# Local output projection moved into the feed-forward pipeline, its neighbours' weights loaded and folded at other points

## The reference

```python
# local attention: o = per-head attended values (4, 1024, 512), window of 128 tokens
x = layernorm(x + (o @ Wo.T + bo))                 # its output projection
# strided cross attention: 16 heads, 4 keys per head and batch, out of the 64 context rows
x = layernorm(x + strided_attention(x, ctx))
# feed-forward with blockwise FP4 rounding q() of input, hidden and weights, 512 -> 1408 -> 512
h = silu(q(x) @ q(w_gate).T) * (q(x) @ q(w_up).T)
x = layernorm(x + q(h) @ q(w_down).T)
```

## Time and profile before

| | us |
|---|---|
| median of 3 runs | 3055.73 (3054.52 to 3055.9) |
| profiled execution, its own time | 3053.7 |
| its span | 3052.0 |
| PE busy | 2701.3 (89%) |
| DVE, ACT, POOL busy | 1879.7, 846.6, 724.7 |
| last PE instruction of `local_attention` starts | 1748.6 |
| projection's first and last matmul start | 1772.5, 1882.0 |
| first gate matmul starts | 1954.1 |

### The profile page before, as it was taken

How to read it: one execution, slowest core, us unless ns; L and a number is a source line. 1 busy time by engine, 2 the same in 40 slices (tenths; PEclk the granted TensorE clock), 3 DMA queues, 4 the chain that set the end, 5 groups by cost and what they waited for, 6 DMA issues and landing times. The chain is left out here.

```text
span 3052.0 us, 40234 instructions
## 1 busy us (share of the span) xinstructions
PE 2701.3 (89%) x14516; PEld 1393.4 (46%) x14516; DVE 1879.7 (62%) x3509; ACT 846.6 (28%) x1360; POOL 724.7 (24%) x703
## 2 busy tenths in 40 slices
PE   8999578888698899578887787899999999999997
PEld 4444344555344455234444433444444444444443
DVE  4786366676346344267777656366676676667664
ACT  1111122222122233266767500222222222222210
POOL 1322035454100233355555333000000000000000
PEclk9999799999899899789999998899999999999999
DMA  5332300000111333322222254300000000000000
GB/s 168 123 129 73 114 14 28 14 27 0 73 42 41 94 103 97 97 59 80 82 79 80 63 162 139 116 4 11 7 8 11 7 8 7 11 7 7 8 11 11
DMA packets 188413, 168.94 MB, mean 55 GB/s; under 512 B 28328, under 2 KB 141480, under 8 KB 187216
## 3 DMA queue, kind: packets, MB, share of 16 engines
q1 hardware_dynamic: 176888, 155.71, 16.1%
q10 hardware_dynamic: 11352, 10.94, 1.1%
HBM read 90.37 MB, written 50.99 MB: 46 GB/s over the span
## 5 line engine op out<-in xcount | busy, mean ns | idle before, releaser
L2099 PE MATMUL bank<-tl_WdT,tl_HT 128*128 128x512 f32 x704 | 321.7, 598 | 10.6 <-ACT tl_HT L2154 10.6
L2075 PE MATMUL bank<-tl_WgT,tl_XQT 128*128 128x512 f32 (+1 forms) x768 | 322.2, 563 | 0.0
L2080 PE MATMUL bank<-tl_WuT,tl_XQT 128*128 128x512 f32 (+1 forms) x768 | 317.9, 557 | 0.0
L2032 POOL TENSOR_TENSOR tl_rs<-tl_ve,mhalf 128x1 f32<-128x1 f32 x32 | 17.4, 545 | 948.5 <-DVE tl_ve L2211 948.5
L2264 DVE TENSOR_TENSOR tl_HH<-bank,tl_SG 128x512 f32<-128x512 f32 (+1 forms) x96 | 62.1, 647 | 277.9 <-PE bank L2080 277.9
L1477 POOL TENSOR_SCALAR_AFFINE_SELECT la_TR<-la_TR 128x512 f32<-128x512 f32 x256 | 171.6, 674 | 229.7 <-ACT la_TR L1650 189.0
L2080 PEld LDWEIGHTS bank<-tl_WuT,tl_XQT 128*128 128x128 f32 x768 | 145.9, 190 | 156.4 <-issue 122.5
L2075 PEld LDWEIGHTS bank<-tl_WgT,tl_XQT 128*128 128x128 f32 x768 | 142.5, 192 | 136.0 <-issue 110.5
L2099 PEld LDWEIGHTS bank<-tl_WdT,tl_HT 128*128 128x128 f32 x704 | 126.9, 191 | 141.8 <-issue 141.8
L2139 ACT ACTIVATE tl_SG<-bank 128x512 f32<-128x512 f32 (+1 forms) x96 | 53.9, 562 | 411.7 <-PE bank L2075 411.7
L1706 DVE SCALAR_TENSOR_TENSOR la_TR<-la_TR,bank 128x1024 f32<-128x1024 f32 (+1 forms) x128 | 141.6, 1148 | 2.4 <-PE bank L1559 2.1
(11 more groups left out here) (312 smaller groups left out, 4892.9 us busy)
## 6 DMA issues: line engine op xcount, KB each, us to landing
fp_weights<-ssm_WS ACTq DMA_DIRECT2D x33, 256.0 KB, 2.0
ssm_xT<-in_x_T SPq DMA_DIRECT2D x8, 1024.0 KB, 6.6
X<-in_x SPq DMA_DIRECT2D x8, 1024.0 KB, 8.8
xa_XS<-X SPq DMA_DIRECT2D x8, 1024.0 KB, 4.7
l_XS<-X SPq DMA_DIRECT2D x8, 1024.0 KB, 4.7
v<-la_VS SPq DMA_DIRECT2D x32, 256.0 KB, 2.3
unit_g<-la_GH SPq DMA_DIRECT2D x32, 256.0 KB, 2.8
unit_gT<-la_GT SPq DMA_DIRECT2D x32, 256.0 KB, 3.2
```

Of the source, the lines that this page charges most:

```text
L2075: mm = e.matmul(bank[(2 * q) % 3][:, 0:w], XQT[n % 2][:, c, :], WgT[:, x // P:(x + w) // P, c, :], start=(c == 0), stop=(c == C - 1))
L2080: mm = e.matmul(bank[(2 * q + 1) % 3][:, 0:w], XQT[n % 2][:, c, :], WuT[:, x // P:(x + w) // P, c, :], start=(c == 0), stop=(c == C - 1))
L2099: mm = e.matmul(bank[DOWN][:, :], HT[:, q, :], WdT[:, q, :], start=(q == 0), stop=(q == IC - 1))
```

## The change

1. A new stage `folded_weights` comes second (after `prepare`, ahead of `ssm`). It is the old folding block, plus the fold of the local value bias into the local output bias (4 matmuls of 128x512), and it stores what it made in DRAM (`SW`, 1.4 MB in two DMAs). It has 17 counters.
2. `local_attention_output` is gone. Its projection (`local_out`, 4 matmuls a tile), add and statistics (`local_sum`), `pow` (POOL) and normalisation (`local_normal`) are in the pipeline, three tiles ahead of the gate: `local_out(s + 3)` stands between the second and third piece of gate and up. It shares bank `VOUT` with `attend`, so `attend(s + 2)` waits for `local_sum(s + 3)`, and `local_out(n)` waits for `attended_sum(n - 2)`. The bias is added on POOL one tile earlier. The slots begin at -3. SP loads an attended tile (256 KB) a slot, two buffers.
3. The 1/129 is applied where `local_attention_projections` copies the values (the same instruction, with a scale).
4. `TR` becomes a tile that lasts until the end. The feed-forward weights go into its freed parts, issued by SP in `local_attention` at rounds 114 (2.1 MB), 118 (2.1 MB), 120 (1.6 MB) and 128 (2.9 MB); the last pair is stored in round 130. The pipeline waits for these semaphores, which are cleared at the very end.
5. The hidden tile is made in `HQ` itself (`SG` and `HH` are gone); the instructions are the same.

The loads of the feed-forward weights, in SP's program of `local_attention` (the call stands at the end of each round):

```diff
+LAST_IN = (3, 7, 10, 17)
...
+                def feed_forward_weights(s):
+
+                    for n, last in enumerate(LAST_IN):
+                        x = NS - RING + last
+                        if s == (x + 3) // 2 * 2:
+                            e.wait_ge(s_pv.sem, s_pv.at(x + 1))
+                            if n < NP:
+                                c, w = PIECES[n]
+                                for r, at in enumerate((GATE_AT[n], UP_AT[n])):
+                                    e.dma_start(k.tiles[:, at:at + C * w].rearrange("p (i d) -> p i d", d=D),
+                                                units[r][:, c // P:(c + w) // P, :]).then_inc(k.d_w[n], 16)
+                            else:
+                                e.dma_start(k.tiles[:, DOWN_AT:DOWN_AT + IC * D].rearrange("p (i d) -> p i d", d=D),
+                                            units[2]).then_inc(k.d_wd, 16)
```

What `folded_weights` has beyond the old folding block (SP, then PE), and SP's first loads in the last stage:

```diff
+                e.dma_start(lWoT[:, :, :], chunked(a["L1_attn_Wo_T"])).then_inc(s_lw.sem, 16)
+                e.wait_ge(s_m2.sem, s_m2.at(C + 1))
+                e.dma_start(k.SW[:, M2_AT:VO_AT], MQ[:, :]).then_inc(s_out.sem, 16)
+                e.wait_ge(s_vo.sem, s_vo.at(B // 2 + 1))
+                e.dma_start(k.SW[:, VO_AT:FOLDED], VB[:, :]).then_inc(s_out.sem, 16)
+                e.wait_ge(s_out.sem, s_out.at(32))
...
+                for c in range(C):
+                    mm = e.matmul(bank[7][:, :], lbvr[:, c, :], lWoT[:, c, :], start=(c == 0), stop=(c == C - 1))
+                mm.then_inc(s_fm.sem, 1)
...
+                e.dma_start(WoT[:, :, :], chunked(a["L1_attn_Wo_T"])).then_inc(s_wo.sem, 16)
+                load_attended(0)
+                e.dma_start(VB[:, :], k.SW[:, VO_AT:FOLDED]).then_inc(s_wb.sem, 16)
+                load_attended(1)
+                e.dma_start(MQ[:, :], k.SW[:, M2_AT:VO_AT]).then_inc(s_wm.sem, 16)
```

The pipeline (PE, then DVE) and the list of stages:

```diff
-        SLOTS = range(-2, NT + 3)
+        SLOTS = range(-3, NT + 3)
...
+                def local_out(n):
+                    if n == 0:
+                        e.wait_ge(s_wo.sem, s_wo.at(16))
+                    e.wait_ge(s_at[n % 2].sem, s_at[n % 2].at(16 * (n // 2 + 1)))
+                    e.wait_ge(s_a5.sem, s_a5.at(n - 1))
+                    for c in range(C):
+                        mm = e.matmul(bank[VOUT][:, :], AT[n % 2][:, c, :], WoT[:, c, :], start=(c == 0), stop=(c == C - 1))
+                    mm.then_inc(s_lo.sem, 1)
...
                 def attend(n):
                     e.wait_ge(s_pc.sem, s_pc.at(n + 1))
-                    e.wait_ge(s_a5.sem, s_a5.at(n))
+                    if n == 0:
+                        e.wait_ge(s_wb.sem, s_wb.at(16))
+                    e.wait_ge(s_a4.sem, s_a4.at(min(n + 2, NT)))
...
                     if there(s):
                         gate_and_up(s, 1)
+                    if there(s + 3):
+                        local_out(s + 3)
+                    if there(s):
                         gate_and_up(s, 2)
...
                     if there(s - 1):
                         h_scaled(s - 1)
+                    if there(s + 3):
+                        local_sum(s + 3)
                     if there(s):
                         product(s, 2)
                     if there(s + 1):
                         x_quant(s + 1)
+                    if there(s + 3):
+                        local_normal(s + 3)
                     if there(s):
                         h_divide(s)
...
-STAGES = [prepare, ssm, cross_attention, linears, local_attention_projections, local_attention, local_attention_output,
-          strided_attention_and_feed_forward]
+FIRST = [prepare, folded_weights, ssm, cross_attention, linears, local_attention_projections]
+LAST = [local_attention, attention_outputs_and_feed_forward]
```

More of the change, by code:

```diff
@@ L86, in __init__ @@
         self.FW = self.dram("fp4_weights", (UNITS, P, D))
+        self.SW = self.dram("folded", (P, FOLDED))
+        self.done = []
+        self.d_w, self.d_wd = [self.kept(f"ffn_w{q}") for q in range(len(PIECES))], self.kept("ffn_w_down")
         self.GNd, self.VNd = self.dram("unit_g", (B * C, P, T)), self.dram("v", (B * C, P, T))
@@ L301, in _ @@
             e.memset(k.mhalf[:, :], -0.5)
+PIECES = ((0, 512), (512, 512), (1024, FI - 1024))
+SLOT = 2 * GT
+FREED = 8
+RING = 20
+GATE_AT = [(FREED + 4 * q) * SLOT for q in range(3)]
+UP_AT = [(FREED + 4 * q) * SLOT + C * w for q, (_, w) in enumerate(PIECES)]
+DOWN_AT = 0
+NP = len(PIECES)
+LAST_IN = (3, 7, 10, 17)
+M2_AT, QB_AT, VO_AT, BO_AT = 0, C * B * S2, (C + 1) * B * S2, (C + 1) * B * S2 + B // 2 * D
+FOLDED = BO_AT + D
 def blocks(x):
@@ L1343, in local_attention @@
         sem = lambda n: k.tick("la2_" + n)
-        TR = [sb(f"TR{n}", [P, HC, WIN]) for n in range(RING)]
+        TR = [k.tiles[:, n * SLOT:(n + 1) * SLOT].rearrange("p (h q) -> p h q", h=HC) for n in range(RING)]
         GN, VN = ([sb(f"{m}{n}", [P, P]) for n in range(TILES)] for m in ("GN", "VN"))
@@ new lines, in _ @@
+                for n, (t, bias) in enumerate(((KG, bk), (VG, bv))):
+                    for m in range(C):
+                        e.wait_ge(s_km.sem, s_km.at(C * n + m + 1))
+                        for j in range(HC):
+                            q = slice(DH * j, DH * j + DH)
+                            x = bank[C * n + m][q, 0:B * S2].rearrange("p (b m h) -> p b m h", b=B, h=H)[:, :, :, HC * m + j]
+                            i = e.activation(t[q, m, :, HC * m + j, :], x, ACT.Identity, bias=bias[q, m:m + 1])
+                        i.then_inc(s_kv.sem, 1)
@@ L1878, in _ @@
-                st.chain.end()
-def strided_attention_and_feed_forward(k):
+                    e.tensor_scalar(bqr[:, c, :], k.ones[:, :], bq[:, c:c + 1], None, ALU.mult).then_inc(s_bq.sem, 1)
+                e.wait_ge(s_lb.sem, s_lb.at(32))
+                for c in range(C):
+                    e.tensor_scalar(lbvr[:, c, :], k.ones[:, :], lbv[:, c:c + 1], None, ALU.mult).then_inc(s_lr.sem, 1)
+                e.wait_ge(s_bo.sem, s_bo.at(16))
+                e.tensor_scalar(bo[:, :], bo[:, :], 1.0 / H, None, ALU.mult).then_inc(s_bs.sem, 1)
@@ L2337, in build, with _ @@
         k = Kernel(nc, ctx, a, out)
-        for stage in STAGES:
+        for stage in FIRST:
             k.stage(stage)
+        k.tiles = k.sb(ctx, "tiles", [P, RING * SLOT])
+        for stage in LAST:
+            k.stage(stage)
+        with nc.Block() as block:
+            @block.sync
+            def _(e):
+                for s in k.done:
+                    e.sem_clear(s)
 _PLAIN = ["x", "L0_attn_b_in", "L0_attn_A", "L0_attn_Cm", "L0_attn_b_gate", "L0_attn_b_out",
```

294 lines of the change are left out of this document (139 added, 155 removed).

## The result

The changed kernel took 3068.68 us (median of 5 runs, 3066.65 to 3070.8); the kernel before, run beside it, 3055.85 (5 runs, 3054.52 to 3058.1). The ratio is 1.0042, 95% interval 1.0028 to 1.0057: **slower by 0.42%**, 12.8 us. The profiled execution took 3066.65 with a span of 3064.9, which is 12.9 above the 3052.0 of before. The time lies in the range of 3046 to 3071, near its upper end, and nearest to rivals B (3066.3) and D (3069.6), while the likeliest single forecast was 3059.7.

What follows compares the result with a forecast made beforehand. It took PE to set the slot, with DVE having at least 8.6 us to spare in each. Terms 21.8 + 36.8 + 1.0 + 99.8 + 49.7 = 209.1 against 205.1, +4.0 on 3055.7, gave 3059.7 us; range 3046 to 3071.

Steps and rivals of the forecast that it cites:

- B: Attention's last rounds: weight loads keep `VN` back twice, 7.6 us in place of 1.0, so 3066.3; chance 0.25.
- D: Slots: one more 0.34 us wait in each of 29, for `local_sum` or the attended tile: 3069.6; chance 0.08.
- the likeliest single forecast: Whole kernel: 4.0 us slower, 3059.7, within the 0.2% that measurement can tell from none; chance 0.47.
- the sum (+4.0): Whole change: five terms make 209.1 us against 205.1 before, so 4.0 us slower.
- Projection in the slots, 99.8: Pipeline slots: 29 tiles projected at 3.44 us each add their full length on PE, 99.8 us.
- E: Slots: the projection fills the 0.34 us that PE waits in each, 9.9 us less: 3049.8; chance 0.03.
- Folding, moved to the front, +49.7: Front of the kernel: the new folding stage makes the old first stage start issuing at 51.9 instead of 2.19, +49.7 us.
- The weights' effect inside the attention, 1.0: Attention's last rounds: weight loads issued ahead of `VN` keep it back, 1.0 us in all; bounds 0 and 7.6.
- From the attention's end to the first `local_out`, 21.8: Gap after the attention's last matmul: PE starts `local_out` 21.8 us later; bounds 16.3 and 24.
- the term for the store held behind the down weights: Attention's end: the last attended store, queued behind 2.9 MB of down weights, lands at 1757.5 instead of 1752.0, 5.5 us lost.
- Filling, 36.8: First `local_out` to first gate: three tiles projected ahead, 36.8 us against 21.0 before; bounds 32 to 42.
- C: Seams cheaper: store slips past weights (-5.5), fill projections run warm (-4.5), no `VN` wait (-1.0): 3048.7; chance 0.17.

Runs made afterwards that it cites:

- run 5: Changed kernel with the projection a stage of its own again, folding in front and early weights kept; 3082.65 us, ratio 1.0083.
- Experiment 2: Changed kernel with only the down weights moved to the last stage, gate and up loads left in the attention's rounds; 3062.68 us, ratio 1.0021.
- run 6: Changed kernel with 59 extra 128x128 products of ones put into PE's waits in the fill; 3060.23 us, ratio 1.0017.
- run 1: Changed kernel with all feed-forward weights loaded in the last stage, none in the attention's rounds; 3058.24 us, ratio 1.0004.
- Run 10: Changed kernel with weights loaded late, last stage's first loads before its counters, tile 0 quantised before `local_sum(2)`, first four biases added early; 3048.73 us, ratio 0.9976.
- run 9: Changed kernel with the output biases of the first four tiles added on POOL before the slots; 3066.84 us, ratio 1.0039.
- run 11: Run 10's kernel with 59 extra 128x128 products of ones put into PE's waits in the fill; 3051.92 us, ratio 0.9988.

## Why the prediction was right, and where it was off

The predicted direction of the sum (+4.0) was right, its size a third of what came, and 0.47 had been put on a change that no measurement would show. That the time fell into the range is in part luck: it was widened up to D's value, and D's longer slots did not come; of B's 7.6 us 4.2 came, and the largest other part, 4.0 in the fill, is in no rival. By its steps:

- **Projection in the slots, 99.8**: right, 99.4. No wait for `local_sum` or for an attended tile stands in any slot from 2060 on, so D and E are out.
- **Folding, moved to the front, +49.7**: right, 50.0, with first `ssm` load of ACT at 52.48 (forecast 52; the working's last 0.5, from 51.4 to 51.9, has no row). What was not drawn out is that the old place kept a seam: folding alone cost some 14 us net (run 5), which is as much as the fusion gained.
- **The weights' effect inside the attention, 1.0**: this step failed. Its mechanism was right, its size was wrong. It let 2.1 MB pass in 5.4 us from issue and had `VN` land at about 1736, 0.7 late; in the trace the piece's two loads landed 5.5 and 9.2 us after issue, and the pair behind them 7.5, so that it came 3.84 too late, with 0.4 more for matmuls at a granted clock of 0.50 behind it. That is rival B's sum for one wait (7.3 after issue, 3.8 too late). What had been held against B, that most of a piece has drained by the next round's `VN`, did not hold: `VN` went out 2.8 us after the piece, when at most 0.5 MB of it had moved (124, 116 and 338 GB/s in the three microseconds from 1779). B had the wait twice, and it came once. Experiment 2 puts all that hangs on the pieces at 4.4.
- **From the attention's end to the first `local_out`, 21.8**: off by 1.8, and the whole of it is the term for the store held behind the down weights, 5.5 forecast, 9.0 - 1.7 = 7.3 measured. The estimate took 2.9 MB at 387 GB/s; the weights themselves needed 11.2 us from issue to landing. Experiment 2 gives 7.1 for it by the time of the whole kernel.
- **Filling, 36.8**: this step failed, by 4.0, most of it by the clock. The steps of the working against the timeline: `local_out(0)` +0.5, add to normalised +0.9 (the collision with POOL), transposes and scores of tile 0 +1.2, `local_out(1)` +1.6 (6.08 for 4.5), weights' transpose to the next x transpose -0.2, transposes and scores of tile 1 -0.7, `local_out(2)` +0.9 (5.35 for 4.5), sum -0.2, quantising and the rest to 0.1. No run shows the 4.5 for the second and third `local_out`: in the trace of after they took 6.08 and 5.35 us, in run 6, with the waits filled, 3.65. The three projections add twelve matmuls to the fill, and with PE's waits between them the granted clock went from 0.56 to 0.71 only; in run 6 it was 1.00. That run shows both that the clock was the cause of most of the 4.0 and that C's warm fill, 32.3 by its terms, was there to be had (31.9), but not by the twelve matmuls alone. The 0.9 of the collision with POOL is a term that the prediction did not have.

So the loss of 12.8 us is: weights early +11.5, from run 1, and 1.3 for all the rest, within noise of nothing. In that rest stand fusing, about -13, and folding moved, about +14, a split that rests on run 5. The early weights were meant to hide loads that the last stage hides anyway.

## What to carry to other kernels

Before a load is moved ahead, look for the wait that it would remove; if there is none, the move can only cost, and what it costs is in the small transfers issued behind it (here a 64 KB operand and a 128 KB store, together 11.5 us). A stage that is moved takes its seam along and may leave one behind: price both ends. And edits that each shorten a fill need not add up. Run 10's four did; the fillers written into waits did not: when another edit moves a wait, the filler stays and becomes work on the path.

## What the hardware showed that was not expected

- A 128 KB store behind 2.9 MB in the same queue landed after 9.0 us instead of 1.7, a 64 KB load behind 2.1 MB after 7.5 instead of 1.8. With the weights in ACT's queue SP still waited 5.0 for the store instead of 1.3.
- A VectorE `TENSOR_SCALAR` over 128x512 took 1.48 us instead of 0.55 when a GpSimd addition of 1.26 had begun 0.07 us before; the next one, at 1852.38, did so too, and took 0.55 in run 9 without the addition. Waiting to the end of the addition, 1.19 us after DVE's start, and then running as in run 9 would make, as an estimate, 1.19 + 0.55 = 1.74; the 1.48 is less, so the trace shows a long wait but not quite a full one. What the two engines wait for in each other no run shows.
- Work put in a long wait of PE did not start at full speed: in run 11, the 48 instructions of the first 24 products, at a granted clock of 0.66 on the average and 0.50 from 1811 to 1815, took 8.19 us, 0.17 each; in run 6, the 28 at 1833.89, at 1.00, took 3.29, 0.12 each.
